# Edge-type codes of a two-layer graph network: 16 full products against 16 pairs of 64-column products

## The reference

```python
def _build_mask(edge_index, edge_type, edge_type_weights, dtype):
    src, dst = (edge_index[0], edge_index[1])
    w = jax.nn.softplus(edge_type_weights)
    mask = jnp.full((N, N), -jnp.inf, dtype=dtype)
    mask = mask.at[src, dst].set(w[edge_type - 1])
    ...
scores = jnp.einsum('hnd,hmd->hnm', q2, k2) * scale + mask[None]
attn = jax.nn.softmax(scores, axis=-1)
```

## Time and profile before

| | |
|---|---|
| median of 3 runs | 226.34 us |
| lowest and highest | 225.06 and 229.69 us |
| profiled execution, its own time | 226.81 us |
| its span | 224.6 us |
| PE busy | 215.9 us of the span, 4789 products |
| granted TensorE clock of the core | 1.0 |

### The profile page before, as it was taken

The page is one execution under the profiler, slowest core; times in us unless marked ns, Lnnn a source line. Parts: engine busy times, 40 slices in busy tenths (PEclk is TensorE's granted clock), DMA queues, the critical chain, the costliest instruction groups (busy, mean ns, idle before and its releaser), DMA issues.

```text
span 224.6 us, 10191 instructions
## 1 busy us (share of the span) xinstructions
PE 215.9 (96%) x4789; PEld 210.0 (94%) x4789; DVE 84.9 (38%) x150; ACT 22.4 (10%) x41; POOL 22.9 (10%) x53
## 2 busy tenths in 40 slices
PE   2999999999999999999999999999999999999994
PEld 2889989999999999799999999999999999999993
DVE  2459819151499830558978600000000000000624
ACT  2641000000030120221224000000000000000101
POOL 2271003700000000010000860000000000000000
PEclk9999999999999999999999999999999999999999
DMA  6999999999999999999999999999999999996002
GB/s 212 385 391 425 417 420 410 393 385 355 353 398 343 350 362 356 371 376 365 384 413 381 358 400 362 382 374 368 330 347 371 356 359 362 368 382 276 3 3 70
DMA packets 14684, 77.01 MB, mean 343 GB/s; under 512 B 4874, under 2 KB 5138, under 8 KB 5428
## 3 DMA queue, kind: packets, MB, share of 16 engines
q1 hardware_dynamic: 14112, 75.96, 88.5%
q10 hardware_dynamic: 532, 0.42, 0.7%
HBM read 75.97 MB, written 0.39 MB: 340 GB/s over the span
## 4 chain that ended last, share of the span: by engine, by line
PE 95%; DMA 2%; DVE 1%; issue 0%; ACT 0%
PE acc L788 82%; PE acc L1033 4%; DMA x_sb<-in_x 2%; PE turn L976 1%; PE side L836 1%; PE side L976 1%; PE side L1033 1%; PE turn L864 1%; DVE stats L505 1%; PE acc L806 1%; PE turn L880 0%; PE side L847 0%; PE turn L847 0%; PE acc L880 0%; PE side L829 0%
## 5 line engine op out<-in xcount | busy, mean ns | idle before, releaser
L788 PE MATMUL acc<-mean,raw 128*64 128x96 f32 x2048 | 85.5, 246 | 0.4 <-issue 0.2
L788 PEld LDWEIGHTS acc<-mean,raw 128*64 128x64 f32 x2048 | 84.8, 137 | 0.9 <-issue 0.8
L788 PE MATMUL acc<-hT,raw 128*64 128x96 f32 x1024 | 44.2, 247 | 0.4 <-issue 0.4
L788 PEld LDWEIGHTS acc<-hT,raw 128*64 128x64 f32 x1024 | 42.8, 137 | 1.4 <-issue 1.1
L751 DVE TENSOR_TENSOR uT<-acc,uT 128x384 f32<-128x384 f32 x2 | 1.1, 558 | 82.3 <-PE acc L788 82.3
L788 PE MATMUL acc<-qT,raw 128*64 128x96 f32 x512 | 21.7, 246 | 0.0
L788 PE MATMUL acc<-kT,raw 128*64 128x96 f32 x512 | 21.7, 246 | 0.0
L788 PEld LDWEIGHTS acc<-kT,raw 128*64 128x64 f32 x512 | 21.3, 137 | 0.3 <-issue 0.3
L788 PEld LDWEIGHTS acc<-qT,raw 128*64 128x64 f32 x512 | 21.2, 137 | 0.2 <-issue 0.2
L788 PE MATMUL acc<-uT,raw 128*64 128x96 f32 x256 | 13.5, 276 | 0.0
L788 PEld LDWEIGHTS acc<-uT,raw 128*64 128x64 f32 x256 | 13.0, 159 | 0.3 <-ACT uT L409 0.2
(11 more groups left out here) (176 smaller groups left out, 150.8 us busy)
## 6 DMA issues: line engine op xcount, KB each, us to landing
raw<-in_weights SPq DMA_DIRECT2D x284, 256.0 KB, 4.8
raw<-in_weights SPq DMA_DIRECT2D x1, 1024.0 KB, 6.3
x_sb<-in_x ACTq DMA_DIRECT2D x1, 192.0 KB, 3.7
x_sb<-in_x SPq DMA_DIRECT2D x1, 192.0 KB, 3.5
out<-out_rows SPq DMA_DIRECT2D x1, 192.0 KB, 2.1
out<-out_rows ACTq DMA_DIRECT2D x1, 144.0 KB, 2.4
out<-out_rows SPq DMA_DIRECT2D x1, 48.0 KB, 2.2
bias_rows<-in_biases ACTq DMA_DIRECT2D x1, 36.0 KB
```

Of the source, the lines that this page charges most:

```text
L788: mm = pe.matmul(a[g * HD:(g + 1) * HD, b, c * N:(c + 1) * N], raw[:, s, at:at + HD], moving(k0 + k), start=opens and k0 == 0 and c == 0 a ...
```

## The change

show_codes makes each 96-column product into two of 64 stationary columns, the second of which writes PSUM partitions 64 to 127 (of which 96 to 127 get zeros, and nothing reads them). So that the second has 64 columns, src_hot gets 128 columns for each chunk in place of 96. POOL fills columns 96 to 127 with zeros once, ahead of key_mul, and PE waits for that with the new semaphore src_padded. one_hot and count take the first 96 columns.

```diff
-        src_hot = sb("src_hot", [EP, EC, N], F16)
+
+        src_hot = sb("src_hot", [EP, EC, P], F16)
...
             inverse_root()
 
+            gp.memset(src_hot[:, :, N:P], 0.0).then_inc(src_padded, 1)
+            gp.wait_ge(src_padded, 1)
             step(gp.memset(key_mul[:, :], 1.0))
...
-            one_hot(src_hot, src_f, src_hot_ready)
+            one_hot(src_hot[:, :, 0:N], src_f, src_hot_ready)
...
                     pe.wait_ge(src_hot_ready, 1)
+                    pe.wait_ge(src_padded, 1)
                     pe.wait_ge(dst_hot_ready, 1)
                 for j in range(EC // 2):
                     c = r * EC // 2 + j
-                    mm = pe.matmul((side, turn)[r][0:N, j // CH, (j % CH) * N:(j % CH + 1) * N], src_hot[:, c, :],
-                                   dst_hot[:, c, :], start=True, stop=True)
+                    for g in range(2):
+                        part = slice(g * HD, (g + 1) * HD)
+                        mm = pe.matmul((side, turn)[r][part, j // CH, (j % CH) * N:(j % CH + 1) * N],
+                                       src_hot[:, c, part], dst_hot[:, c, :], start=True, stop=True)
                 mm.then_inc(codes_shown, 1)
...
-                pe.matmul(side[0:N, 0, 0:TW], src_hot[:, c, :], rel_hot[:, c, :], start=c == 0,
+                pe.matmul(side[0:N, 0, 0:TW], src_hot[:, c, 0:N], rel_hot[:, c, :], start=c == 0,
```

More of the change, by code:

```diff
@@ L191, in gnn_kernel @@
         row_ready = sem("row_ready")
+        src_padded = sem("src_padded")
         iota_made = sem("iota_made")
```

## The result

The changed kernel takes 228.52 us (median of 16 runs, 226.2 to 230.9), the one before 226.87 us in the same comparison (16 runs, 224.95 to 230.37). The ratio is **1.0065, with an interval of 1.0034 to 1.0095**: some 1.5 us slower, where I forecast 0.28 us less. The ratio compares only runs within 1.5% of their kernel's fastest, 12 of the changed kernel's 16. The profiled execution has a span of 225.7 us and a time of 227.51 us.

The account below looks back on a forecast made before the run. PE was taken to bound the kernel: its codes go from 1.00 to 0.72 us, -0.28 us, with 0 on the rest. The median was to go from 226.34 to 226.1 us, range 225.0 to 228.0 us.

Parts of the forecast that it names:

- The cost of the 16 products now: Codes on PE: 0.49 + 0.36 us, plus 0.15 us coming back to pairs, 1.00 us with the switches of form.
- the switch belongs to the type: Rival: f16 codes between f32 pieces cause the 0.13 and 0.15 us, so the change does nothing, 226.3 us; chance 0.09.
- The cost of the pairs: Codes on PE as 16 pairs, members side by side, at 45 ns each: 0.72 us, bounds 0.66 to 1.44 us.
- a price for each product: Rival: each of the codes' 32 products holds up the next some 25 ns, 0.80 us, change -0.20 us; chance 0.25.
- The instruction limit: Rival: PE takes at most 48 instructions per microsecond, codes 1.32 us, change +0.32 us; chance 0.15, shared with members in sequence.
- test of the sign: On the codes' rows: the forecast gain would have the wrong sign if a pair took over 62 ns (1.00/16).
- The fill on POOL: Zeros on POOL ahead of key_mul: 0.45 us, hidden by the edge cast's 4.38 us wait for data, so no cost.
- the one-hot: DVE's pass writing 1536 elements, now with gaps: 1.75 us, at worst 1.75 us more, within 3.08 us idle; PE unaffected.
- the transfers' lead over PE: Weights land ahead of PE, which is some 5 us behind its data at piece 8; PE doesn't wait for them.
- the memset holds up the edge chain: Rival: POOL's fill delays edge cast, keys and codes; 2% slower needs about 15 us; chance 0.01 with anything else taking microseconds.
- The 2% bound: Whole kernel: time stays within 2% of before, chance 0.97; faster by over 2% 0.01, slower 0.02.

Follow-up runs that it names:

- d3: The kernel before, with the codes' products as pairs of 64 and 32 columns, without padding or fill: ratio 1.0236 (1.0183 to 1.0288).
- b1: The kernel before, with SP waiting ahead of piece n until piece n-2 has landed, so fewer weight transfers are queued: ratio 1.1414 (1.1348 to 1.148).
- c4: The kernel before, unchanged, run once more: ratio 0.9992 (0.9954 to 1.003).

## Why the prediction was wrong, step by step

**The cost of the 16 products now (1.00 us): right.** The gaps of 0.13 and 0.15 us vanish in the pair form, and the switch is a matter of form, not of type: f16 pairs between f32 pieces pay nothing. The rival "the switch belongs to the type" falls. The rule of the Trainium skill that I had set beside it (TensorEngine Tiling (Array Packing), Key Properties) holds as well.

**The cost of the pairs (0.72 us): right, a little too high.** 42.5 ns a pair, 0.68 us. The rival "a price for each product" falls: two products in 42.5 ns are 21 ns each. The Trainium skill (TensorE: Matmul & The Clock Gate, "Wait — 56ns, not 53.3ns?") says that start-to-start never drops below some 25 ns; the trace disagrees for members of a pair, which start 10 and 33 ns apart by turns, and the measurement decides.

**The instruction limit: named, and dismissed on a poor argument.** This is the step that failed first: the path behind the codes was taken to cost nothing more than before. I had the signs on the table: a rate never above 48 instructions to the microsecond in the trace, and two "issue" gaps. I took the columns' pace as proof that supply didn't matter, though that only shows that supply suffices for the pieces. It suffices barely: a block of pieces lasts 5.28 us, and in the block that holds the codes its successor is there 4.2 to 6.1 us after the boundary (the transfer's start, 1.8 to 3.8 us, and 2.35 us), behind the queued weights. The rival was also mis-sized: as a rate over the codes alone it gave +0.32 us; as a block that ends too soon it is 0.9 us lost for 0.3 us saved, +0.6 us. The loss comes 36 products later, in work that the change doesn't touch, so a price of the edited rows alone can't find it. The prediction's own test of the sign, a pair of over 62 ns, looked at these rows too, and with 42.5 ns it saw nothing.

**The fill on POOL (nothing): wrong, and this was the other failed step.** Its size was right (0.52 us against 0.45), and so was its cover on POOL. I asked who waits for POOL and never who works beside it. One pass of DVE went from 0.34 to 1.11 us and the first piece began 0.65 us later, in all four traces with the fill at this place, and in none of those without. As a rule PE also reached its full pace later. The first pieces run at the lower of the two clock levels, 1.2 and 2.4 GHz: 64 products took 5.26 us in the trace before, at half the later pace of 2.64 us. The clock records begin with the rise, which came at 12.2 to 13.6 us in the four traces with the fill and at 9.7 to 12.9 us in twelve without it. The ranges overlap, and between the first two traces the order is the other way. That the rise came later because of the idle PE is argued from the times alone; no run held the clock fixed.

The Trainium skill (SBUF — State Buffer, "SBUF: two separate sides") says that DVE and GpSimd have one pair of ports in common, that a DVE instruction in a two-port mode, or in some cases one with two inputs in SBUF, and a GpSimd instruction lock it for their whole length, and that the one which starts second is blocked fully. The trace agrees in part: DVE's pass stood until 0.14 us after the fill's end. But by the records the blocked pass started first (6.34 against 6.79 us), and no view shows in which mode it ran. Had I weighed this rule, the fill would have been a rival of its own, at about 0.5 us.

**The rest:** the one-hot took 1.75 us, no other wait appeared, and the transfers' lead over PE held. The rival "the memset holds up the edge chain" was right about the instruction and wrong about the victim. The range (225.0 to 228.0 us) missed the median by 0.5 us: it had been widened for the scatter of the runs, not for a loss of 1.5 us. The 2% bound, for which 0.97 was given, held.

## What to carry to other kernels

Where an engine is busy without a gap, ask how its instructions arrive: if a block is used up faster than the next can come through a full transfer queue, time saved by short instructions is taken back at the block's end, far from the edit. So gaps named "issue" are worth counting in instructions from one to the next, before the edit. And an operation on an idle POOL can cost DVE: here a fill of 102 x 512 did, while the operation of 96 x 1 that runs beside the same passes before (L338) left them at 0.34 us. Put fills where both engines are idle, here right behind the iota.

## What the runs showed of the hardware that I had not expected

- A pair of f16 products of 64 stationary and 96 moving columns takes 42.5 ns, a full product of 96 columns 45 ns. A second product of 32 columns in place of 64 makes it 0.15 us for each product (d3), and in that trace the granted clock fell for 3.4 us behind them.
- PE's instructions come in blocks of some 256 (37 transfers of 16 KB for 9,640 instructions), which hold 127 or 128 products with their loads. The transfer starts 0.4 to 3.9 us after a boundary in the blocks between 18 and 55 us, and PE goes on some 2.35 us after its start where it had to wait. With fewer weights queued (b1) it starts 0.9 to 2.2 us after it.
- The waits at these boundaries are part of the scatter between runs: in the trace of the kernel before PE lost 0.6, 0.3 and 0.4 us at three of them, in its repeat c4 0.5 us at one near 90 us and little elsewhere; the spans were 224.6 and 223.2 us. The place at which the clock rises, 12.9 and 12.45 us there, is another part.
- With the weights' transfers limited to four to eight of 256 KB under way the rate fell from 343 to 299 GB/s.
